# Routed groups of a mixture-of-experts layer taken two at a time on TensorE, with gathers ahead of scatters

## Chip, cores and metric

The kernel runs on one core of a Trainium2 chip. The metric is device time in microseconds (us) of one execution; lower is better. TensorE's granted clock in the profiled execution is 0.993 of 2.4 GHz on average, and 1.00 in the stage that the change touches.

## The reference

A small vision tower with one layer: 16 images of 96x96, 37 tokens each (T = 592 tokens, width 256), float32. Patch embedding, a transformer block (16 heads, low-rank projections), a layer norm, and then the feed-forward part that matters here, a mixture of experts:

```
logits = xt @ gate_w.T                      # 15 experts
scores = softmax(logits);  topk_w, topk_idx = top_k(scores, 3);  topk_w /= sum(topk_w)
h = xt @ fc1_w[e].T + fc1_b[e]              # 256 -> 512, halves xh and g
a = gelu(g) * xh * geglu_mult[e]            # 256
yexp = a @ fc2_w[e].T + fc2_b[e]            # 256 -> 256
y = sum over the token's 3 experts of topk_w * yexp
ys = a shared expert of width 512, for every token
out = layernorm(x + y + ys)
```

## The kernel before

Everything up to the shared expert runs first (about 138 us). Then come the routed experts. Their 1776 token rows are sorted by expert into 42 half groups of 64 rows; two half groups make a group of 128 rows, so there are NT = 21 groups. The upper half of group i belongs to expert i (from group 15 on, to a copied set of weights), the lower half to an expert that is read from a table at run time. Each group goes through a chain over all engines:

1. POOL, `gather(i)`, L556 to L562: an indirect DMA reads the group's 128 token rows from DRAM into one of NXG = 6 buffers `xg` (inside embed_sb). It waits until the transpose of group i-6 has read the buffer.
2. PE, `tile_transposed(i)`, L1641 to L1647: two transposes of 128x128 float32 into PSUM bank 6 + i % 2.
3. ACT, `tile_in(i)`, L742 to L747: copies them to `xT` (in cT), two buffers.
4. PE, `first(i)`, L1663 to L1681: the first products. Two bf16 matmuls add the bias (96 rows x 64 columns, 512 moving), then eight float32 matmul instructions (128x64, 512 moving; the instructions of the two halves stand in different columns of the array and run side by side) into bank 4 + i % 2.
5. ACT, `gate(i)`, L749 to L753: gelu of half of the result.
6. DVE, `gated(i)`, L1228 to L1233: the product with the other half into `a_r` (in h1), two buffers; it waits until the transpose of group i-2 has read the buffer.
7. PE, `gated_transposed(i)`, L1683 to L1691: two transposes into bank 2 + i % 2.
8. DVE, `gated_in(i)`, L1235 to L1240: copies them to `aT` (in cT), two buffers; it waits until the second products of group i-2 are done.
9. PE, `second(i)`, L1693 to L1701: the second products, eight float32 instructions (128x64, 256 moving) into bank i % 2.
10. ACT, `tile_out(i)`, L755 to L759: copies the result to one of NYS = 4 buffers `ys` (in ln_mem); it waits until the scatter of group i-4 has left the buffer.
11. POOL, `scatter(i)`, L564 to L572: an indirect DMA writes the rows to `y_dram`, sorted by token.

Each engine has its own queue, in order, written out by hand; semaphores tie them together. The queues before are: PE takes in each turn first(i), second(i-2), tile_transposed(i+1), lower_expert(i+1), gated_transposed(i-1) (L1706 to L1718). `lower_expert(i)` (L1651 to L1653) is a value load: PE's sequencer reads an expert's number from SBUF into a register that addresses the weights. ACT takes gate(i), tile_out(i-2), tile_in(i+1) and, from i = 4 on, one `diagonal` (L761 to L765, a scaled copy of the identity for the final sum; L767 to L777). DVE takes gated(i), gated_in(i-1), and in the first three turns parts of the softmax of the gate (`softmax_end`, `weigh`, `choose_weights`; L1242 to L1252). POOL takes six gathers, then scatter(i), gather(i+6) (L576 to L581).

SP copies the weights for the last six groups (L453 to L457); copy k waits for the first products of group 2k, and first(15) waits for all copies (L1673). After the last scatter, SP reads all rows back from y_dram (L459 to L461), PE adds them up over the diagonals (L1720 to L1737), and DVE and ACT do the final layer norm.

## Time and profile before

| | us |
|---|---|
| median of 3 runs | 240.78 (240.02 to 243.75) |
| the profiled execution, its own time | 240.42 |
| its span, first to last instruction | 238.6 |
| PE busy | 220.6 (92%) |
| ACT busy | 95.5 |
| DVE busy | 98.5 |
| POOL busy | 107.1 |
| bias of group 0 to bias of group 20 | 138.84 to 213.77 |

Times in the rows are counted from the first instruction of the span. PE is TensorE's matmul stream and PEld its weight loads; PEldq is the sequencer in front of them. Ends of matmuls are modelled, so a start is a firmer number than an end. A float32 transpose or matmul stands under the line of its helper: L344 is every matmul, L1646 the transposes of gathered rows, L1690 those of the gated rows. `stage`, `f1v`, `xn`, `h` and `f2u` as weights in the rows of the last groups are the copies. 1.8 us of the profiled time lie outside the span.

### The profile page before, as it was taken

What the parts mean: (1) busy time and instruction counts of PE and PEld (TensorE: products, weight loads), DVE (VectorE), ACT (ScalarE), POOL (GpSimd) and SP (SyncE); (2) the same over time, 40 slices, a digit from 0 to 9 for tenths busy, and PEclk for the clock granted to TensorE, in tenths of its full rate; (3) what the DMA queues carried; (4) which work ended last, traced back from release to release, by engine and by line L of the source; (5) the groups of instructions that cost most, each with busy time, mean ns of one, the idle gap of its engine ahead of it and who ended that gap; (6) DMA issues with size and microseconds to landing.
All of it is one profiled execution on the core that took longest, in us unless ns stands there. A gap on an engine that the chain in (4) does not pass through costs nothing.

```text
span 238.6 us, 4515 instructions
## 1 busy us (share of the span) xinstructions
PE 220.6 (92%) x1605; PEld 142.4 (60%) x1605; DVE 98.5 (41%) x261; ACT 95.5 (40%) x215; POOL 107.1 (45%) x149
## 2 busy tenths in 40 slices
PE   7999899888997899999999989999999999999991
PEld 4776577677776577777877734444444444444670
DVE  3155432679962521243678845222222212121043
ACT  2003546476782694345231523243433424333132
POOL 0130028388420699999900360644546464333100
PEclk9999999999997999999999999999999999999999
DMA  7999999000004980000110040398435222201552
GB/s 234 400 347 390 347 413 414 28 4 3 3 0 150 420 355 0 3 0 3 44 58 0 26 110 3 99 325 320 168 119 198 66 69 66 66 25 44 180 193 81
DMA packets 11648, 34.43 MB, mean 144 GB/s; under 512 B 2426, under 2 KB 4139, under 8 KB 11628
## 3 DMA queue, kind: packets, MB, share of 16 engines
q1 hardware_dynamic: 9612, 28.65, 32.0%
q0 software_dynamic: 2016, 5.51, 7.6%
q8 instruction: 13, 0.21, 0.4%
q14 instruction: 7, 0.06, 0.1%
HBM read 25.43 MB, written 4.01 MB: 123 GB/s over the span
## 4 chain that ended last, share of the span: by engine, by line
PE 84%; ACT 8%; issue 3%; DVE 2%; DMA 2%; ACTq 0%
PE ps L344 76%; ACT cT L746 3%; PE ps L1646 3%; PE ps L1445 2%; DMA embed_sb<-embed 2%; ACT pair_mem L679 1%; ACT pair_mem L673 1%; PE ps L1455 1%; DVE ln_mem L848 1%; ACT xn L605 0%; PE ps L1563 0%; PE ps L1399 0%; PE ps L1327 0%; DVE ln_mem L835 0%; ACT ln_mem L588 0%
## 5 line engine op out<-in xcount | busy, mean ns | idle before, releaser
L344 PE MATMUL ps<-wres,cT 128*64 (+1 forms) x360 | 63.8, 465 | 0.4 <-DVE cT L1239 0.4
L344 PEld LDWEIGHTS ps<-wres,cT 128*64 128x64 f32 (+1 forms) x360 | 26.2, 131 | 29.2 <-issue 24.2
L568 POOL DMA_INDIRECT y_dram<-ln_mem,dest_i x21 | 20.8, 989 | 40.0 <-ACT ln_mem L759 39.7
L559 POOL DMA_INDIRECT embed_sb<-x_dram,gather_i x21 | 20.7, 986 | 20.5 <-DVE gather_i L1164 14.4
L1232 DVE TENSOR_TENSOR h<-ps,h 128x256 f32<-128x256 f32 x21 | 8.9, 425 | 47.1 <-issue 31.0
L529 POOL TENSOR_SCALAR wres<-wres,mult 128x256 f32<-128x256 f32 x30 | 27.1, 915 | 0.0
L753 ACT ACTIVATE h<-ps 128x256 f32<-128x256 f32 x21 | 8.1, 385 | 42.4 <-PE ps L344 38.3
L357 POOL TENSOR_TENSOR wres<-wres,cst_sb 128x148 f32<-128x148 f32 x24 | 10.9, 481 | 23.2 <-DVE wres L868 20.8
L344 PE MATMUL ps<-h,stage 128*128 128x296 f32 x64 | 17.7, 417 | 0.0
L344 PE MATMUL ps<-bias_t,fac_mem 96*64 96x512 bf16 x42 | 8.5, 403 | 5.8 <-ACT cT L746 5.3
L490 POOL TENSOR_TENSOR wres<-wres,cst_sb 128x111 f32<-128x111 f32 x32 | 11.1, 378 | 6.1 <-PE ps L1455 6.1
L344 PE MATMUL ps<-embed_sb 128*128 128x288 f32 (+1 forms) x63 | 13.5, 375 | 0.2 <-DMA embed_sb<-embed 0.2
L344 PEld LDWEIGHTS ps<-h,stage 128*128 128x128 f32 x64 | 11.7, 190 | 3.2
L1239 DVE COPY cT<-ps 128x256 f32<-128x256 f32 x21 | 8.8, 425 | 11.1 <-PE ps L1690 11.1
L344 PE MATMUL ps<-xn,wres 128*128 128x296 f32 x48 | 13.1, 419 | 0.0
L759 ACT ACTIVATE ln_mem<-ps 128x256 f32<-128x256 f32 x21 | 8.1, 385 | 11.2 <-PE ps L344 10.7
L344 PEld LDWEIGHTS ps<-embed_sb 128*128 128x128 f32 (+1 forms) x63 | 10.3, 179 | 3.7 <-DMA embed_sb<-embed 0.8
L598 ACT ACT_TABLE_LOAD x9 | 11.5, 1283 | 1.3 <-DVE eps_t L800 1.1
L699 ACT ACTIVATE embed_sb<-ps,vec_sb 128x296 f32<-128x296 f32 x16 | 7.9, 504 | 9.0 <-PE ps L344 9.0
L344 PE MATMUL ps<-embed_sb,f1v 128*128 128x296 f32 x32 | 10.8, 424 | 0.2 <-ACT embed_sb L699 0.2
L344 PEld LDWEIGHTS ps<-xn,wres 128*128 128x128 f32 x48 | 8.8, 190 | 3.2 <-issue 0.9
L344 PE MATMUL ps<-embed_sb,f2u 128*128 128x296 f32 x32 | 10.3, 412 | 0.0
(194 smaller groups left out, 393.0 us busy)
## 6 DMA issues: line engine op xcount, KB each, us to landing
wres<-experts SPq DMA_DIRECT2D x15, 768.0 KB, 13.6
embed_sb<-embed SPq DMA_DIRECT2D x6, 416.0 KB, 5.4
wres<-ut SPq DMA_DIRECT2D x3, 768.0 KB, 9.2
stage<-shared SPq DMA_DIRECT2D x2, 771.0 KB, 13.6
wres<-y_dram SPq DMA_DIRECT2D x4, 384.0 KB, 4.5
stage<-wres SPq DMA_DIRECT2D x2, 512.0 KB
f1v<-fc_v SPq DMA_DIRECT2D x1, 512.0 KB
f2u<-fc_u SPq DMA_DIRECT2D x1, 512.0 KB
```

The costliest lines, as they stand in the source:

```text
L344: return nc.tensor.matmul(o, w, x, start=start, stop=stop)
L357: return eng.tensor_tensor(kblk[:, par, u, c], kT[:, c, bass.ds(p * (2 * S) + u * S, S)].unsqueeze(1).to_broadcast([P, HR, S]), cst[:, C_B ...
L490: pool.tensor_tensor(vst[:, par, c, u].rearrange("p (r s) -> p r s", r=G3), vT[:, c, bass.ds(p * (2 * S) + u * S, S)].unsqueeze(1).to_broa ...
L529: pool.tensor_scalar(w[:, f * D:(f + 1) * D], w[:, f * D:(f + 1) * D], factors[:, f:f + 1], None, ALU.mult).then_inc(scaled, 1)
L559: pool.indirect_dma_start(out=xg[:, i % NXG], out_offset=None, in_=x_dram[:, :], in_offset=bass.IndirectOffsetOnAxis(ap=gather_i[:, column ...
L568: pool.indirect_dma_start(out=y_dram[:, :], out_offset=bass.IndirectOffsetOnAxis(ap=dest_i[:, column(i):column(i) + 1], axis=0), in_=ys[:, ...
L598: nc.scalar.activation(warm_t[:, i:i + 1], eps_t[:, 0:1], function)
L699: nc.scalar.activation(hm[:, f], ps[:, HM_BANK + g % 2, 0:HT], ACT.Gelu_apprx_tanh, bias=vec[:, C_FC1B + f:C_FC1B + f + 1]).then_inc(hm_do ...
L753: nc.scalar.activation(gel_r[:, i % 2], ps[:, 4 + i % 2, F:2 * F], ACT.Gelu).then_inc(ge_done, 1)
L759: nc.scalar.activation(ys[:, i % NYS], ps[:, i % 2, 0:D], ACT.Copy).then_inc(ys_done, 1)
L1232: nc.vector.tensor_tensor(a_r[:, i % 2], ps[:, 4 + i % 2, 0:F], gel_r[:, i % 2], ALU.mult).then_inc(a_done, 1)
L1239: nc.vector.tensor_copy(aT[:, i % 2].rearrange("p f s -> p (f s)"), ps[:, 2 + i % 2, 0:F]).then_inc(at_done, 1)
```

## The change

The four queues are rewritten to take two groups in a turn. PE takes first(j), first(j+1), then tile_transposed of j+2 and j+3 (each followed by its lower_expert), gated_transposed of j-2 and j-1, and second of j-4 and j-3, for j = 0, 2, ..., 20. The second products thus come two pairs behind the first ones, where they were two groups behind. After the loop come second(18), gated_transposed(20) after second(19), and second(20). ACT, DVE and POOL follow in the same order. On POOL gather(i+6) now stands ahead of scatter(i-4), where scatter(i) stood ahead of gather(i+6). No operation is added or taken away.

```diff
--- before.py
+++ after.py
@@ -576,9 +576,12 @@
             for i in range(NXG):
                 gather(i)
             for i in range(NT):
-                scatter(i)
                 if i + NXG < NT:
                     gather(i + NXG)
+                if i >= 4:
+                    scatter(i - 4)
+            for i in range(NT - 4, NT):
+                scatter(i)
@@ -765,16 +768,18 @@
             tile_in(0)
-            for i in range(NT):
-                gate(i)
-                if i >= 2:
-                    tile_out(i - 2)
-                if i + 1 < NT:
-                    tile_in(i + 1)
-                if 4 <= i < 4 + TOPK * TT:
-                    diagonal(i - 4)
-            tile_out(NT - 2)
-            tile_out(NT - 1)
+            tile_in(1)
+            for j in range(0, NT, 2):
+                for i in range(j, min(j + 2, NT)):
+                    gate(i)
+                for i in range(j + 2, min(j + 4, NT)):
+                    tile_in(i)
+                for i in range(max(j - 4, 0), max(j - 2, 0)):
+                    tile_out(i)
+                for q in range(max(j - 4, 0), min(max(j - 2, 0), TOPK * TT)):
+                    diagonal(q)
+            for i in range(NT - 3, NT):
+                tile_out(i)
             warm(ACT.Sqrt)
@@ -1239,15 +1244,15 @@
-            for i in range(NT):
-                gated(i)
-                if i >= 1:
-                    gated_in(i - 1)
-                if i == 0:
+            for j in range(0, NT, 2):
+                for i in range(j, min(j + 2, NT)):
+                    gated(i)
+                for i in range(max(j - 2, 0), j):
+                    gated_in(i)
+                if j == 0:
                     softmax_end()
-                if i == 1:
                     weigh()
-                if i == 2:
+                if j == 2:
                     choose_weights()
             gated_in(NT - 1)
@@ -1701,20 +1706,23 @@
             pe.wait_ge(own_done, 2)
-            lower_expert(0)
-            tile_transposed(0)
-            for i in range(NT):
-
-                first(i)
-                if i >= 2:
-                    second(i - 2)
-                if i + 1 < NT:
-                    tile_transposed(i + 1)
-                    lower_expert(i + 1)
-                if i >= 1:
-                    gated_transposed(i - 1)
+            for i in range(2):
+                lower_expert(i)
+                tile_transposed(i)
+            for j in range(0, NT, 2):
+
+                for i in range(j, min(j + 2, NT)):
+                    first(i)
+                for i in range(j + 2, min(j + 4, NT)):
+                    tile_transposed(i)
+                    lower_expert(i)
+                for i in range(max(j - 2, 0), j):
+                    gated_transposed(i)
+                for i in range(max(j - 4, 0), max(j - 2, 0)):
+                    second(i)
+            second(NT - 3)
+            second(NT - 2)
             gated_transposed(NT - 1)
-            second(NT - 2)
             second(NT - 1)
```

## Rows read from the trace of the kernel before

**Rows 1.** The page, busy time (share of the span) and instructions of each engine.
```profile
PE 220.6 (92%) x1605; PEld 142.4 (60%) x1605; DVE 98.5 (41%) x261; ACT 95.5 (40%) x215; POOL 107.1 (45%) x149
```

**Rows 2.** Chain that ended last, routed stage: start us, us, what.
```profile
148.61 2.99 PE ps L344 x18
...
213.33 0.39 ACT cT L746
213.77 2.99 PE ps L344 x18
```

**Rows 3.** Timeline of group 19: start us, us, engine line op, [idle before <- releaser].
```profile
209.94 0.41 PE L344 MATMUL ps<-bias_t,fac_mem 96*64 96x512 bf16 x2 [0.26 <-ACT cT L746]
210.18 0.59 PE L344 MATMUL ps<-wres,cT 128*64 x1
...
211.89 0.38 PE L344 MATMUL ps<-wres,cT 128*64 x1
...
212.54 0.38 PE L344 MATMUL ps<-wres,cT 128*64 x1
...
212.86 0.44 PE L1646 MATMUL ps<-cst_sb,embed_sb 128*128 128x128 f32 x2
...
213.13 0.38 PE L1690 MATMUL ps<-cst_sb,h 128*128 128x128 f32 x2
213.33 0.38 ACT L746 ACTIVATE cT<-ps 128x256 f32<-128x256 f32 x1
```

**Rows 4.** One line's instructions, the gated transposes: duration ns min/median/max.
```profile
L1690 PE MATMUL ps<-cst_sb,h x42: 272/273/328, 144.1 to 217.1; 128*128 128x128 f32 x42
```

**Rows 5.** Timeline of the end of the stage, columns as in rows 3.
```profile
216.69 0.66 PE L1690 MATMUL ps<-cst_sb,h 128*128 128x128 f32 x4
...
217.16 0.76 DVE L1239 COPY cT<-ps 128x256 f32<-128x256 f32 x2 [0.38 <-PE ps L1690]
...
217.73 0.42 PE L344 MATMUL ps<-wres,cT 128*64 x1 [0.39 <-DVE cT L1239]
...
218.64 0.38 PE L344 MATMUL ps<-wres,cT 128*64 x1
...
219.72 0.38 ACT L759 ACTIVATE ln_mem<-ps 128x256 f32<-128x256 f32 x1 [0.48 <-PE ps L344]
...
220.23 0.71 PE L344 MATMUL ps<-cst_sb,hs 128*128 128x128 f32 x4
220.79 0.97 POOL L568 DMA_INDIRECT y_dram<-ln_mem,dest_i  x1 [0.30 <-issue]
...
220.87 0.69 PE L344 MATMUL ps<-b_sb,comb 17*128 17x256 f32 x2
```

**Rows 6.** Timeline of the first groups, columns as in rows 3.
```profile
137.99 0.38 PE L1646 MATMUL ps<-cst_sb,embed_sb 128*128 128x128 f32 x2
...
138.84 0.41 PE L344 MATMUL ps<-bias_t,fac_mem 96*64 96x512 bf16 x2 [0.47 <-issue]
...
140.90 0.44 PE L1646 MATMUL ps<-cst_sb,embed_sb 128*128 128x128 f32 x2
141.02 0.38 ACT L753 ACTIVATE h<-ps 128x256 f32<-128x256 f32 x1 [2.23 <-issue]
```

**Rows 7.** PE's sequencer, the value load L1653: all, group 0, group 20 (last row).
```profile
L1653 PEldq TENSOR_LOAD <-owner_i x21: 297/309/942, 136.9 to 210.7; - x21
...
L1653 PEldq SEQ_ASSERT  x1: 32/32/32, 137.7 to 137.7; - x1
...
L1653 PEldq SEQ_ASSERT  x1: 18/18/18, 211.4 to 211.4; - x1
```

**Rows 8.** One line's instructions, POOL's gathers: duration ns min/median/max.
```profile
L559 POOL DMA_INDIRECT embed_sb<-x_dram,gather_i x21: 945/973/1169, 134.2 to 203.4; - x21
```

**Rows 9.** SP's last issue of a weight copy, columns as in rows 3.
```profile
178.34 0.51 SPq L457 DMA_DIRECT2D h<-wres  x1
```

**Rows 10.** DMA of 138 to 238.6 us in 40 equal slices.
```profile
GB/s 101 111 7 1 12 108 197 345 293 380 348 131 64 325 143 52 333 136 52 52 104 57 54 104 52 52 103 54 0 59 52 0 52 104 232 314 184 55 101 88
```

## Prediction

> **What bounds the kernel now.** I read the page first: PE is busy for 92% of the span, every other engine for less than half [rows 1]. So only time in which PE stands or changes over can be gained, unless another queue starts to hold PE back. Next, the chain of work that ended last. In the routed stage it repeats one pattern, 18 matmul instructions on PE (2.99 us), two transposes, then the copy L746 on ACT (0.39 us), then PE again. From group 3 (148.61) to group 20 (213.77) there are 17 periods, 65.16 / 17 = 3.83 us each [rows 2]. ACT is thus on the path once per group, though it is 40% busy.
>
> The timeline of one group shows where the 3.83 us go [rows 3]. From the bias at 209.94 to the first product 0.24 us; four pairs of first products to 211.89, 1.71 us; four pairs of second products, whose last starts at 212.54, so 0.65 / 3 = 0.215 us each and 0.86 for all. That is 2.81 us of products. The transposes start at 212.86, 0.10 us later than the next product would have (212.54 + 0.215 = 212.76). The copy L746 starts at 213.33, ends at 213.71, and the next bias starts at 213.77. PE had idled 0.26 us by then. Sum: 2.81 + 0.10 + 0.44 (two transposes) + 0.03 + 0.38 + 0.06 = 3.82.
>
> **The change part by part.** I count in the time t of a turn of two groups, 0 at bias(j).
>
> *Products.* The same instructions: 2 x (0.24 + 1.71) = 3.90 us for first(j) and first(j+1), 2 x 0.86 = 1.72 us for two seconds [rows 3]. No gain, no loss.
>
> *Change-over to the transposes.* One per pair instead of one per group, 0.10 us each [rows 3].
>
> *Transposes.* Four in a row take 0.66 us from the first start to the last end [rows 5], one of them 0.27 [rows 4], so the fourth starts 0.39 after the first. The first is followed after 0.17, later ones after 0.11 (in rows 3 the third starts 0.27 after the first and the two after it span 0.38 - 0.27 = 0.11). Eight in a row: 0.17 + 6 x 0.11 = 0.83 from first to last start. What was 2 x 0.66 becomes 1.10 to the last end.
>
> *Change-over from the transposes to second().* Rows 3 show none of these without a wait. It lies between 0.11 us after the last transpose's start (no cost at all) and 0.27 + 0.15 = 0.42 (all run out, and a first weight load that nothing hides, as the wait of 0.14 from DVE's end, 217.59, to PE's start, 217.73, in rows 5). A near row is the end of the kernel: from float32 matmuls of 128 moving columns on 128 rows, started at 220.23 and spanning 0.71, the last starts at about 220.67 and the 17-row matmul at 220.87 [rows 5], 0.20 us. I take 0.21, 0.10 above no cost, like the other direction. From second() to a bias, and from first() to a bias, no tile width changes; I take 0 and at most 0.10 for each.
>
> The Trainium skill (TensorEngine Tiling, Key Properties) says that a change of tiling mode, not just of the tile, drains TensorE. Rows 3 nearly agree, since the transpose starts 0.06 before the modelled end of the product ahead of it (212.54 + 0.38). By that rule the way back would cost 0.27 instead of 0.21, and the forecast would be some 0.5 us later; the rule also speaks for the change, which halves the number of drains.
>
> *Sum.* 3.90 + 0.10 + 0.83 + 0.21 + 1.72 = 6.76 us for two groups, against 7.66. I use 6.77. With both ends of the unknowns it is 6.66 to 7.18.
>
> *What hides the ACT copies.* gate(j+1) follows its bias by 2.18 us [rows 6], t = 1.95 + 2.18 = 4.13 to 4.52. tile_in(j+2) then runs to 4.93, tile_in(j+3) to 5.32. bias(j+2) comes at 6.77, so 1.8 us of cover: the wait of 0.26 per group is gone. Four gated transposes and two seconds are that cover. Where it is missing, at j = 0 and j = 2, the wait stays (below).
>
> *DVE.* gated(j) needs `a_r` free, that is gated_transposed(j-2), which now stands behind first(j+1): its end is t = 4.00 + 0.61 + 0.27 = 4.88, so gated(j) runs to 5.34 (0.43 each, rows 5) and gated(j+1) to 5.80. First(j+2) at 6.77 needs the former. gated_in(j-2) waits for second(j-4), t = 5.04 + 1.08 = 6.12, and ends at 6.55; gated_in(j-1) ends 0.6 us into the next turn. Their readers come at 5.04 of the turn after. What is late next is gated(j) with 1.4 us of slack.
>
> *POOL.* A DMA costs 0.97 us plus 0.30 between two [rows 5]; two gathers and two scatters per pair are 4 x 1.28 = 5.1 us of 6.77; with the longest gather in all four places, 1.17 + 0.30 [rows 8], 5.9. gather(j+9) waits behind scatter(j-2), which waits for tile_out(j-2) in the next turn, at t = 6.77 + 6.5 = 13.3; its transposes run in turn j+8, four turns on, at t = 4 x 6.77 + 4 = 31. tile_out(i) needs a buffer scattered two turns earlier. Cost 0.
>
> *Value loads.* From 136.9 to 137.7 one takes PE's sequencer 0.8 us [rows 7]. Now two stand close together, 1.6 us in the sequencer with 0.22 us of transposes between. Before, the load for group 20 was over at 211.4 [rows 7] while its transposes started at 212.86 [rows 3]: the sequencer was 1.4 us ahead of the array with one load done. In the new order it is let go at t = 5.32 of the turn before, when xT is filled, and needs its next transposes out 5.4 us later. I take 0.
>
> *Weight copies.* The last is issued at 178.34 [rows 9], and the DMA falls back from 333 GB/s within the slices to 183.3 [rows 10], 5 us later. In the new order first(10) is done near 172, and first(15), which waits for the copies, comes near 185.4 (turn times as below: bias(10) at 149.6 + 3 x 6.77, bias(15) at 149.6 + 5 x 6.77 + 1.95). Cost 0.
>
> *Start.* The order is now load(0), transposes(0), load(1), transposes(1), first(0). transposes(0) start at 137.99 and bias(0) at 138.84 [rows 6]; the load for group 0 ends at 137.7 [rows 7], so load(1) ends near 138.5, transposes(1) run from about 138.8, and bias(0) comes at 139.15. That costs 0.3 us (0 to 0.6, the gather of group 1 being about as late). First(0), first(1): to 143.05. Four transposes from 143.15; tile_in(2) waits for gate(1) and ends at 144.08; bias(2) at 144.13, 0.4 us of wait. First(2), first(3), eight transposes from 148.14; gated_transposed(0) ends at 149.02, gated(2) on DVE at 149.48, and first(4) waits for it: bias(4) at 149.6. From there every turn is full: bias(20) at 149.6 + 8 x 6.77 = 203.8, against 213.77 [rows 2].
>
> *End.* In exchange more is left: before, two seconds and a pair of transposes, now second(16) to second(20). After bias(20): first 1.95, change-over 0.10, four transposes to the last start 0.39, 0.21 back: second(16) starts at 206.42. Four seconds, 3.44; change-over 0.10; gated_transposed(20), 0.44; gated_in(20), 0.03 + 0.43 + 0.14 [rows 5], which nothing covers now, where second(19) covered it before. second(20) starts at 211.0, against 218.64 [rows 5]: 7.6 us earlier. POOL's last five scatters come 0.86 us apart but take 1.28: the first can start at 206.42 + 1.08 + 0.38 + 0.03 = 207.9, the last at 213.0, against 220.79 [rows 5]: 7.8 us earlier. The reading back and the final sum start from these two, so all moves by 7.7. Profiled execution: 240.42 - 7.7 = 232.7. The median of the runs lies 0.36 above that execution, so 233.1.
>
> **The rivals.**
>
> 1. *The change-overs cost more.* Transposes to second at 0.42 and 0.10 at each of two other edges: up to 0.4 us per pair, 9 pairs, 3.7 us more, 236.8. For it: the 17-row matmuls near the end, which start 0.20 apart from their neighbours. Against it: bias to first products, another change of rows, costs 0.24 - 0.21 = 0.03 [rows 3].
>
> 2. *The wait only changes its name.* The 0.26 us return elsewhere, as PE's wait for gated(j), which now hangs on a transpose late in the turn, or on second() for gated_in. If both savings are lost, 9 turns x 0.9 = 8 us come back: 240.8. For it: exactly this happens at j = 2. Against it: 1.4 us of slack in full turns.
>
> 3. *Slower: the value loads.* They stand in PE's own queue. If the sequencer can't run further ahead than the array's last few instructions, both are exposed, 1.6 us per pair over 8 full turns, 12.8 us: 245.9. It decides once the sequencer's lead at tile_transposed(j+2) is under 1.6 us. Against it: a lead of 1.4 us left after a load, that is over 2 us before it [rows 3, 7].
>
> The Trainium skill (TensorE: Matmul & The Clock Gate, the table of the engine) gives the engine's queue a depth of 64. The products of one group are fewer instructions than that, and by this rule rival 3 would not come up at all.
>
> **How the numbers follow.** The forecast has 0.80 (its own range 231.9 to 234.6), rival 1 0.12, rival 2 0.05, rival 3 0.03. A measurement of this kernel can tell about 2% from no change, 4.8 us, so faster means under 236.0. The forecast and a third of rival 1 lie there: 0.84. Within 2%: most of rival 1 and rival 2, 0.13. Slower: 0.03. The range for 8 in 10 goes from 231.0 (no change-over cost at all, 9 x 0.11 = 1.0 us, a free start, and the spread of the runs) to 236.4 (most of rival 1).
>
> **What would show it right or wrong.** Right: bias starts of even groups 6.7 to 6.9 us apart from group 4 on, no idle time of PE put down to L746 but at groups 2 and 4; transposes in runs of eight, 1.1 us; second() 0.2 us after the last transpose starts; last scatter near 213. Rival 1 shows as turns of 7.0 us or more with no wait behind them, rival 2 as PE idle behind DVE's L1232 or L1239, rival 3 as gaps after the transposes put down to issue, next to a TENSOR_LOAD. The forecast is wrong if turns are longer than 7.1 us or if the last scatter is later than 217.

## The result, and the profile after

| | before | after |
|---|---|---|
| runs beside each other, median (lowest to highest) | 242.26 us (240.02 to 243.9) | 232.69 us (232.08 to 233.6) |
| profiled execution | 240.42 us | 232.10 us |
| its span | 238.6 us | 230.3 us |
| mean granted TensorE clock in it | 0.993 | 0.993 |
| first transposes of the routed stage (us in the span) | 137.99 | 136.13 |
| last scatter starts | 220.79 | 212.53 |
| from there to the end of the span | 17.81 | 17.77 |

Ratio 0.9676, 95% interval 0.9621 to 0.9731: faster. (The ratio leaves out two runs of before, 243.75 and 243.9 us, that count as slow beside its fastest, so it is not the quotient of the two medians.) The forecast was 233.1 us, the median 0.4 below it. But the sum behind it is not that good, and the table shows where. The stage that the change rewrites, from the first transposes to the last scatter, went from 82.80 to 76.40 us, 6.40 less, where the forecast's terms, unrounded, give 7.75 (its text has 7.8, and 7.7 for the whole time). The other 1.86 us lie ahead of it, in code that the change doesn't touch, and they made up for the difference.

The windows view, here the stretch from 65 to 120 us of both kernels (us, busy time and instructions of PE, PEld, DVE, ACT, POOL, granted clock, DMA share, GB/s), first before, then after:

```profile
65.00:120.00 55.00, 52.93 (x358) 39.93 (x358) 22.06 (x59) 28.33 (x54) 41.16 (x44) 0.97 0.27 106
```

```profile
65.00:120.00 55.00, 52.59 (x364) 39.53 (x362) 22.54 (x65) 28.81 (x55) 41.07 (x44) 1.00 0.28 111
```

In the execution of before the granted clock was at its lower level (1.2 GHz) from 74.7 to 78.1 us, in that of after it was not. At half speed for 3.4 us PE does some 1.7 us less, about the 1.86 that are to be explained. The other kernels' profiles agree: of all 12 profiled executions, the five with such a stretch near 74 to 78 us reach the first transposes at 137.99 to 138.38, the seven without it at 135.70 to 136.99. (After has its lower stretch near the end of the span, at no cost: last scatter to end 17.77 against 17.81, so the equal mean clocks of the table mean little.) Such stretches come and go between executions of one kernel, so I compare the kernels below by the stage alone, and give the times beside it.

The stage itself as the chain of work that ended last shows it (start us, us, what):

```profile
141.85 0.95 issue
142.81 4.09 PE ps L344 x20
...
147.35 0.68 ACT cT L749 x2
...
160.34 1.53 another core or an unknown queue
...
162.12 0.39 ACT cT L749
...
173.41 0.59 PE ps L1651 x4
173.99 0.44 PE ps L1695 x4
174.43 5.75 PE ps L344 x36
180.18 0.59 PE ps L1651 x4
```

Where before had a copy on ACT in every period [rows 2], the chain of a full turn is now PE alone: eight transposes, 36 matmul instructions, 180.18 - 173.41 = 6.77 us. PE waits at three places, ahead of bias(2) at 142.81, bias(4) at 148.35 and bias(8) at 162.57, and these views name ACT or `issue` for it. PE's waits in the stage (what waited <- for what: us in all, times, longest), before:

```profile
PE ps L344 <- ACT cT L746: 5.3, 20, 0.5
```

and after:

```profile
PE ps L344 <- issue: 1.0, 1, 1.0
PE ps L344 <- ACT cT L749: 0.9, 2, 0.5
PE ps L344 <- DVE cT L1244: 0.6, 1, 0.6
```

Which of them ACT really ended is told by the starts. first(j+2) waits for two things, the copy tile_in(j+2) on ACT and gated(j) on DVE. Where the copy is the last, as at all the waits of before, the bias follows its end by 0.05 us; so it does at bias(2) (142.75 to 142.81). At bias(4) and bias(8) the copies had ended 0.61 and 0.34 us earlier, and what ended 0.15 us before the bias was gated(2) and gated(6):

```profile
147.78 0.76 DVE L1237 TENSOR_TENSOR h<-ps,h 128x256 f32<-128x256 f32 x2 [3.04 <-PE ps L1695]
...
148.35 0.41 PE L344 MATMUL ps<-bias_t,fac_mem 96*64 96x512 bf16 x2 [0.46 <-ACT cT L749]
```

(Two groups' instructions are merged in the first line; each takes about 0.4 us, and gated(2) ends at 148.21.) So these two waits are DVE's, and the copy on ACT bounds only the first.

The change-over, in the timeline of a full turn of after:

```profile
173.34 0.66 PE L1651 MATMUL ps<-cst_sb,embed_sb 128*128 128x128 f32 x4
...
173.81 0.66 ACT L749 ACTIVATE cT<-ps 128x256 f32<-128x256 f32 x2
173.83 0.60 PE L1695 MATMUL ps<-cst_sb,h 128*128 128x128 f32 x4
174.32 0.42 DVE L1237 TENSOR_TENSOR h<-ps,h 128x256 f32<-128x256 f32 x1 [4.25 <-PE ps L1695]
...
174.36 1.95 PE L344 MATMUL ps<-wres,cT 128*64 x16
...
176.14 0.39 PE L344 MATMUL ps<-bias_t,fac_mem 96*64 96x512 bf16 x2
```

The last transpose starts at 173.83 + 0.60 - 0.27 = 174.16, second(j-4) at 174.36: 0.20 us, where 0.21 was taken. The eight transposes run from 173.34 to 174.43, 1.09 us (1.10 taken). The copy that the bias at 176.14 needs is the first of the two; it ends at 174.20, 1.94 us ahead. gated(10) on DVE starts at 174.32, 0.11 after the modelled end of the transposes that it waits for, and ends 1.39 us ahead of the bias; as the bias follows it by 0.15 where it has to wait, that is a slack of 1.24 us, the smaller of the two.

The end of the stage, and the turn of group 6 in which bias(8) came late, in the same timeline:

```profile
159.13 0.66 PE L1651 MATMUL ps<-cst_sb,embed_sb 128*128 128x128 f32 x4
...
159.62 0.60 PE L1695 MATMUL ps<-cst_sb,h 128*128 128x128 f32 x4
...
161.84 0.66 ACT L749 ACTIVATE cT<-ps 128x256 f32<-128x256 f32 x2 [1.15 <-remote]
162.00 0.76 DVE L1237 TENSOR_TENSOR h<-ps,h 128x256 f32<-128x256 f32 x2 [6.14 <-remote]
...
162.57 0.41 PE L344 MATMUL ps<-bias_t,fac_mem 96*64 96x512 bf16 x2 [0.47 <-ACT cT L749]
...
207.44 0.97 POOL L568 DMA_INDIRECT y_dram<-ln_mem,dest_i  x1 [2.16 <-ACT ln_mem L762]
...
212.53 0.97 POOL L568 DMA_INDIRECT y_dram<-ln_mem,dest_i  x1 [0.30 <-issue]
```

The first of the transposes at 159.13 end, by the model, at 159.5, and PE goes on in order to the gated ones and to second(). Yet ACT gets to copy them only at 161.84, and DVE gets to gated(6), which waits for the gated transposes of group 4 (modelled end 160.00), only at 162.00: both start within 0.2 us of each other, 2.3 and 2.0 us behind their transposes, as if PE's signals for them had been held back. I call this a late signal below, and count it by tile_in unless DVE is named. Over the whole stage tile_in starts 0.04 to 0.16 us after the modelled end of its transposes, except for groups 2 and 3 (0.74 and 1.94) and groups 8 and 9 (2.28 and 2.34). In before it is 0.04 at all 21 groups.

### The profile page after: what moved, and what is told of

Read it like the earlier page. It is cut to its first block, busy times and chain, and to the rows that moved or that the text cites. A ratio compares the mean times of both kernels' runs of the same rounds, so it can differ in the third digit from the quotient of the medians.

```text
span 230.3 us, 4515 instructions
## 1 busy us (share of the span) xinstructions
PE 215.0 (93%) x1605; PEld 140.8 (61%) x1605; DVE 97.1 (42%) x261; ACT 94.5 (41%) x215; POOL 106.7 (46%) x149
## 4 chain that ended last, share of the span: by engine, by line
PE 83%; ACT 5%; DVE 3%; DMA 3%; issue 3%; another core or an unknown queue 1%; POOL 1%; ACTq 0%
PE ps L344 75%; PE ps L1450 3%; PE ps L1651 2%; DMA embed_sb<-embed 2%; PE ps L1695 2%; ACT pair_mem L682 2%; ACT pair_mem L676 1%; DMA embed_sb<-x_dram,gather_i 1%; PE ps L1460 1%; DVE ln_mem L853 1%; ACT xn L608 1%; POOL embed_sb L559 1%; PE ps L1568 0%; ACT cT L749 0%
## 5 line engine op out<-in xcount | busy, mean ns | idle before, releaser
L344 PE MATMUL ps<-wres,cT 128*64 (+1 forms) x360 | 65.9, 468 | 0.6 <-DVE cT L1244 0.6
L1237 DVE TENSOR_TENSOR h<-ps,h 128x256 f32<-128x256 f32 x21 | 8.3, 422 | 45.5 <-PE ps L1695 24.5
L344 PE MATMUL ps<-embed_sb 128*128 128x288 f32 (+1 forms) x63 | 12.8, 362 | 0.3 <-DMA embed_sb<-embed 0.3
L344 PEld LDWEIGHTS ps<-embed_sb 128*128 128x128 f32 (+1 forms) x63 | 9.8, 172 | 3.5 <-DMA embed_sb<-embed 0.8
L1244 DVE COPY cT<-ps 128x256 f32<-128x256 f32 x21 | 8.7, 422 | 7.8 <-PE ps L344 7.8
```

The source lines that it names most:

```text
L344: return nc.tensor.matmul(o, w, x, start=start, stop=stop)
L1237: nc.vector.tensor_tensor(a_r[:, i % 2], ps[:, 4 + i % 2, 0:F], gel_r[:, i % 2], ALU.mult).then_inc(a_done, 1)
L1244: nc.vector.tensor_copy(aT[:, i % 2].rearrange("p f s -> p (f s)"), ps[:, 2 + i % 2, 0:F]).then_inc(at_done, 1)
```

## The experiments

The late signals were the one thing that the forecast had no room for, and there were five questions: do they come back, and at the same groups (a0_again); how much of the gain is the cover of the wait and how much the pairing (e1, e3); does PE's sequencer bound anything (e4); what calls the late signals up (e5, e6, e7, e8); and what the depth of two pairs and the new order on POOL are for (e2, e9). A, B and C in the expectations are the readings that the run was to tell apart. "The stage" is the time from the first transposes of the stage to the last scatter, in the profiled execution.

### a0_again: the changed kernel once more, unaltered

> The changed kernel once more, unaltered, for a second profile. In its first profile two pieces were longer than predicted: bias(0) to bias(2) took 5.61 us (4.98 predicted) and bias(6) to bias(8) 7.42 (6.77), both with ACT starting a copy 1 us or more after its inputs were there. Theory A (a stall tied to the order of the instructions): both come back at the same groups, and the stage from the first transpose (L1651) to the last scatter (L568) is again 76.4 us. Theory B (an accident of one execution): at least one of them is gone or sits at another group, and the stage is 75.2 to 76.0 us.

Stage 76.33 us (76.40 the first time). The turns, from bias(0) on: 5.89, 5.54, 6.79, 7.11, 6.79, 6.77, 6.78, 6.78, 6.77, 6.56. Both long turns come back at the same places, the first and the fourth, as A has it, though not to the same size (5.61 and 7.42 at first), and groups 12 and 13 get a late signal (1.55 and 1.61 us) that costs nothing. The fourth turn also shows that the copy on ACT is not its cause: tile_in(8) starts 0.04 us after its transposes here, while gated(6) starts 1.69 us after its own, and the bias waits for it, this time by the profile's own word:

```profile
163.96 0.75 DVE L1237 TENSOR_TENSOR h<-ps,h 128x256 f32<-128x256 f32 x2 [5.82 <-PE ps L1695]
...
164.53 0.41 PE L344 MATMUL ps<-bias_t,fac_mem 96*64 96x512 bf16 x2 [0.15 <-DVE h L1237]
```

Median of 5 runs 234.48 us against 240.39 before, ratio 0.9812, interval 0.9723 to 0.9901. With an equal stage the time is still 1.8 us above that of the first series. The windows view of the last part of the program says why for the profiled execution (span 235.2), in a0_again and then in after:

```profile
215.00:235.00 20.00, 15.36 (x62) 10.89 (x60) 4.80 (x20) 4.02 (x11) 0.47 (x1) 0.83 0.38 131
```

```profile
213.00:230.00 17.00, 12.27 (x62) 8.78 (x60) 4.81 (x20) 4.08 (x11) 0.50 (x1) 0.91 0.44 154
```

Its clock was lower (0.83) behind the stage, where the last scatter to the end took 20.71 instead of 17.77 us, and lower between 65 and 120 us as in before (0.97). So whole times tell kernels of this family apart by 2 us at best. The stage repeats to 0.1 us here, though partly because its two stalls moved in opposite directions (the first turn 0.28 longer, the fourth 0.31 shorter).

### e1_seconds_last: before, with second() moved behind the transposes

On ACT, tile_in(i + 1) changes places with tile_out(i - 2); on PE:

```diff
                 first(i)
-                if i >= 2:
-                    second(i - 2)
                 if i + 1 < NT:
                     tile_transposed(i + 1)
                     lower_expert(i + 1)
                 if i >= 1:
                     gated_transposed(i - 1)
+                if i >= 2:
+                    second(i - 2)
```

> The kernel before, one group at a time, with second(i-2) moved behind the two pairs of transposes. It covers the wait for ACT's copy L746 and leaves one change-over each way per group. Theory A (the gain has two parts, the wait and the halved change-overs): a group costs 2.81 + 0.10 + 0.39 + 0.21 = 3.51 us instead of 3.83; 18 x 0.32 = 5.8 us less than before, about 0.976 of it, and 1 to 2 us slower than the changed kernel per its full turns. Theory B (pairing is worth nothing beyond the wait): 3.39 us per group, as in the changed kernel. Theory C (the wait comes back elsewhere when one group covers it): 3.7 us or more.

Stage 77.37 us; median 234.26 us, ratio 0.9819, interval 0.9713 to 0.9924. One period of the timeline:

```profile
177.91 0.39 PE L344 MATMUL ps<-bias_t,fac_mem 96*64 96x512 bf16 x2
178.13 1.89 PE L344 MATMUL ps<-wres,cT 128*64 x8
179.94 0.44 PE L1646 MATMUL ps<-cst_sb,embed_sb 128*128 128x128 f32 x2
180.22 0.38 PE L1690 MATMUL ps<-cst_sb,h 128*128 128x128 f32 x2
180.53 1.08 PE L344 MATMUL ps<-wres,cT 128*64 x8
181.45 0.39 PE L344 MATMUL ps<-bias_t,fac_mem 96*64 96x512 bf16 x2
```

3.54 us a group, and no wait at the bias: second() is cover enough for ACT's copy. Nothing else of the change is in this kernel, neither the pairs nor POOL's order, and it already has 82.80 - 77.37 = 5.43 of the 6.40 us. Taking two groups at a time adds the last 1.0. In whole time even that can't be seen: in the same series the changed kernel took 234.48 us (a0_again), this one 234.26. The period is near that of theory A (3.51). It shows no late signal: tile_in starts 0.04 us after its transposes throughout.

### e3_changeover_back: the changed kernel, with two more changes of width per turn

```diff
                 for i in range(j + 2, min(j + 4, NT)):
                     tile_transposed(i)
                     lower_expert(i)
+                if j >= 4:
+                    second(j - 4)
                 for i in range(max(j - 2, 0), j):
                     gated_transposed(i)
-                for i in range(max(j - 4, 0), max(j - 2, 0)):
-                    second(i)
+                if j >= 4:
+                    second(j - 3)
```

> The changed kernel with second(j-4) moved between the gathered rows' transposes and the gated ones: one more change-over each way per turn, all else equal. Theory A (change-overs cost what the rows say: 0.10 into transposes, 0.10 out of them, 0.06 more for the first transpose): turns of 6.78 + 0.26 = 7.04 us, 9 x 0.26 = 2.3 us slower than the changed kernel. Theory B (change-overs cost nothing, only covered waits matter): 6.78 us and the same time. Theory C (TensorE runs empty at each): 7.2 us or more.

Stage 77.77 us, full turns 7.08 us; median 234.79 us, ratio 0.9811, interval 0.9659 to 0.9964.

```profile
180.35 0.66 PE L1651 MATMUL ps<-cst_sb,embed_sb 128*128 128x128 f32 x4
180.93 1.08 PE L344 MATMUL ps<-wres,cT 128*64 x8
181.95 0.66 PE L1695 MATMUL ps<-cst_sb,h 128*128 128x128 f32 x4
182.53 1.08 PE L344 MATMUL ps<-wres,cT 128*64 x8
...
187.43 0.66 PE L1651 MATMUL ps<-cst_sb,embed_sb 128*128 128x128 f32 x4
```

Nothing waits here; a turn is longer by 7.08 - 6.78 = 0.30 us, for one more way into the transposes and one more way out of them. So 0.30 us a turn is what the pairing by itself saves: e1, with 2 x 3.54 = 7.08 us for two groups, pays the same. The stage is only 1.4 us longer than the changed kernel's, not the 2.3 of theory A: eight turns of 0.30 are 2.4, but the fourth has no stall here, which gives back 0.65 (the signals of groups 8 and 9 are 1.62 and 1.66 late and cost nothing), and the rest is at the two ends. The Trainium skill (TensorEngine Tiling, Key Properties) says that a change of tiling mode drains TensorE. The runs agree as far as such a change costs time, 0.30 us for both ways together beyond what the instructions would take in a row; that this time is a drain is not shown.

### e4_loads_doubled: a second value load in front of each

In lower_expert() on PE:

```diff
+                pe.value_load(owner_i[0:1, at:at + 1], min_val=0, max_val=E - 1)
```

> The changed kernel with every value load of PE's sequencer done twice, four per turn (3.2 us of the sequencer, more while the weight copies run, when one load was seen to take up to 1.24 us). Theory A (the sequencer is far enough ahead of the array): turns stay at 6.78 us from group 8 on and the stage from first transpose to last scatter at 76.4 us, but for the first two loads, which stand ahead of the first transposes and cost 0.8 us or so before them. Rival 3 of the prediction (the loads are exposed): turns of 8 us and more, 10 us over the stage.

The turns: 6.26, 5.55, 6.80, 7.24, 7.37, 6.77, 6.78, then 6.78 but for the last, 6.55. Stage 78.13 us; median 235.68 us, ratio 0.9776, interval 0.9690 to 0.9863. In all full turns but one four loads, 4 x 0.8 = 3.2 us in the sequencer, cost nothing (the 7.24 us of the fourth are a late signal's, see below). They cost at the start, 1.73 us from the first transposes to bias(0) instead of 1.05, where the array has no work ahead to hide them, and once more in the fifth turn, 7.37 us, whose copies on ACT start on time. There the weight copies run, one of its four loads takes 1.12 us instead of the median 0.30, and PE stands between the two rows of transposes:

```profile
167.96 0.66 PE L1651 MATMUL ps<-cst_sb,embed_sb 128*128 128x128 f32 x4
...
169.00 0.63 PE L1696 MATMUL ps<-cst_sb,h 128*128 128x128 f32 x4 [0.39 <-issue]
169.56 0.65 PE L344 MATMUL ps<-wres,cT 128*64 x4
```

From the first transpose to second() it is 1.60 us instead of 1.02 (173.34 to 174.36 above), and 0.58 of the turn's extra 0.59 us are that. It is the sign that rival 3 named, a gap put down to `issue` next to a TENSOR_LOAD, in one turn and at twice the loads. With the loads of the changed kernel no turn shows it, though single loads take up to 0.82 us there and 1.24 in a0_again. So rival 3 has fallen for this kernel, but the lead of the sequencer is not without end.

### e5_no_copies: the changed kernel without the weight copies

```diff
-                sp.dma_start(copy_w1[k], wres[:, bass.ds(e * WC, W1C)]).then_inc(ld_copy, 16)
-                sp.dma_start(copy_w2[k], wres[:, bass.ds(e * WC + W1C, W2C)]).then_inc(ld_copy, 16)
...
-                yield slice(TM, P), w1(i, c) if i < E else copy_w1[i - E][:, c * 2 * F:(c + 1) * 2 * F]
+                yield slice(TM, P), w1(i % E, c)
...
-                if i == E:
-                    pe.wait_ge(ld_copy, 32 * NCOPY)
```

SP's copies go, and first() and second() read wres itself. The upper halves of groups 15 to 20 take the weights of experts 0 to 5 in place of the chosen ones; the instructions on PE are as many as before.

> The changed kernel with the twelve weight copies left out; the upper halves of groups 15 to 20 take the weights of experts 0 to 5 instead, so this part of the result is another one. In all profiles so far PE's signals (xT, gated, first products done) came to ACT and DVE up to 2 us behind the modelled ends near 142 to 147 us and near 158 to 162 us. Theory A (the copies' DMA traffic or their semaphore updates hold up the second stall): the turn from bias(6) to bias(8) falls from 7.1 to 7.4 us to 6.78, the first stall stays; stage 0.5 us shorter. Theory B (it has nothing to do with the copies): 7.1 us or more there again.

Stage 75.98 us, turns 5.92, 5.55, 6.79, 6.78, 6.77, 6.78 and so on: the fourth turn, 7.42 and 7.11 in the changed kernel, is a full turn like the others. The first still has its 5.9, and the signals of groups 2 and 3 are late (1.06 and 1.99 us), no others. The timeline at the place of the second stall:

```profile
161.43 0.66 PE L1649 MATMUL ps<-cst_sb,embed_sb 128*128 128x128 f32 x4
161.90 0.66 ACT L747 ACTIVATE cT<-ps 128x256 f32<-128x256 f32 x2
...
164.23 0.39 PE L344 MATMUL ps<-bias_t,fac_mem 96*64 96x512 bf16 x2
```

This is one profile, with whole times of two runs only (232.79 and 236.87 us). But all five other profiles with second() two pairs behind and with the copies (after, a0_again, e3, e4, e6) have late signals behind group 4, and this one has none. So the second stall hangs on the copies, the first on something else.

### e6_late_gathers: the gathers behind the first six held back at the start

In gather(i) on POOL:

```diff
+                if i == NXG:
+                    pool.wait_ge(f1_mm, 4)
```

> The changed kernel with gathers 6 to 9 held back on POOL until first(3) is done (before the change they stood behind the first scatters). Theory A (these four gathers, which the new order lets run at 141 to 145 us, hold up PE's signals at groups 2 and 3): bias(0) to bias(2) falls from 5.6 to 5.9 us to 5.0 to 5.1, stage 0.6 us shorter than 76.4. Theory B (no connection): 5.6 us or more there, and 76.4.

The first turn falls to 4.91 us (forecast 4.98), and no signal of groups 2 and 3 is late. In the other runs of this order the first turn is 4.91 us plus the delay of tile_in(2) beyond its usual 0.04: with 0.70 us of it 5.61 (after), with 0.98 5.89 (a0_again), with 1.36 6.26 (e4). So the first stall has to do with POOL's row of gathers, which in the changed kernel runs on past the first six at one every 1.25 us. But the late signals move rather than go: 2.34 and 2.40 us at groups 6 and 7, 1.30 at group 11, with turns of 7.49 and 7.31. As in a0_again, DVE is the one that PE waits for: bias(6) and bias(10) follow gated(4) and gated(8) by 0.15 us. Theory A is right about the first turn and wrong about the stage: 76.25 us, as good as unchanged; median 235.64 us, ratio 0.9707, interval 0.9610 to 0.9804.

### e2_one_pair_back and e7_one_pair_back_no_copies: second() one pair behind

PE as in the diff, ACT and DVE in the same order, and on POOL gather(i + 6), then scatter(i - 2). e7 is e2 with the weight copies left out as in e5, groups 15 to 20 computed as there.

```diff
                 for i in range(j, min(j + 2, NT)):
                     first(i)
+                for i in range(max(j - 2, 0), j if j < NT - 1 else j - 1):
+                    second(i)
                 for i in range(j + 2, min(j + 4, NT)):
                     tile_transposed(i)
                     lower_expert(i)
-                for i in range(max(j - 2, 0), j):
+                for i in range(j, min(j + 2, NT)):
                     gated_transposed(i)
-                for i in range(max(j - 4, 0), max(j - 2, 0)):
-                    second(i)
...
```

> Pairs, but with the second products one pair back: first(j), first(j+1), second(j-2), second(j-1), transposes of j+2, j+3, then of j, j+1. The eight transposes themselves must cover ACT's copy. Theory A (a turn costs its PE work as long as every copy is covered, and depth only adds filling and emptying): turns of 6.78 us as in the changed kernel, and 1 to 2 us less at the two ends, so 0.992 to 0.996 of the changed kernel. Theory B (the second products are needed as cover): PE waits for L746 or its counterpart in each turn, 7.0 us or more, slower than the changed kernel by 1 to 3 us.

> The kernel with the second products one pair back (turns of 6.63 to 7.56 us, the long ones while the copies run), with the copies left out and the weights of experts 0 to 5 in groups 15 to 20, so that part of the result is another one. Theory A (its eight transposes leave ACT's copy 0.1 us of cover, and the copies' traffic makes signals later than that): without copies all full turns are 6.6 to 6.8 us and the stage is 75.0 us or less, shorter than the changed kernel's 76.4. Theory B (the order itself is too shallow): turns stay above 6.9.

e2: stage 77.15 us, turns of 6.42 to 7.56; median 236.59 us. e7: stage 76.81, turns mostly 6.91 to 6.95; median of two runs 235.87 us, ratio 0.9810, interval 0.9701 to 0.9920. Both come out nearer to B, the order is too shallow (e2's shortest turns, 6.42 to 6.97 us, are not the 7.0 or more that B had). In e2's timeline:

```profile
156.20 0.66 PE L1650 MATMUL ps<-cst_sb,embed_sb 128*128 128x128 f32 x4
...
157.61 0.66 ACT L749 ACTIVATE cT<-ps 128x256 f32<-128x256 f32 x2 [2.63 <-PE ps L1650]
158.04 0.41 PE L344 MATMUL ps<-bias_t,fac_mem 96*64 96x512 bf16 x2 [0.75 <-ACT cT L749]
```

The signal is late by some 1 us and PE stands at the bias for 0.75. With second() ahead of the transposes only the four gated ones cover the copies, and that is 0.11 us: a turn without a late signal takes 6.74 us and its copy ends 0.16 ahead of the bias. All lateness beyond that is paid; in e7 a signal that comes 0.3 us late makes a turn 0.18 longer. In the changed kernel the second products of two groups lie there, 1.7 us. Without the copies (e7) the signals of groups 2 and 3 are still 2.3 us late, those of groups 6 and 7 0.8, and from there to group 17, as long as gathers run, 0.31 to 0.42; from group 18 on it is 0.04 to 0.10. The change's second pair of depth is thus worth 0.8 us of the stage (77.15 - 76.40, and without the copies 76.81 - 75.98), and what it buys is cover against late signals.

### e8_seconds_last_new_pool: e1 with POOL's new order

On top of e1's edits:

```diff
             for i in range(NT):
-                scatter(i)
                 if i + NXG < NT:
                     gather(i + NXG)
+                if i >= 4:
+                    scatter(i - 4)
+            for i in range(NT - 4, NT):
+                scatter(i)
```

> One group at a time with second(i-2) behind the transposes (e1, where ACT's tile_in always started 0.04 us after its transposes and the stage took 77.4 us), and with POOL's queue of the changed kernel: gather(i+6) ahead of scatter(i-4), so that gathers 6 to 9 run early. Theory A (POOL's queue, its run of ten gathers above all, is what makes PE's signals late): tile_in starts 0.5 us or more late at some of groups 2 to 13, as in the changed kernel. Theory B (the pairs on PE are what it takes): 0.04 us at every group, 3.54 us per group, 77.4 us.

Stage 77.38 us, 3.54 a group, tile_in 0.04 us after its transposes at every group: the same as e1. Median 234.53 us, ratio 0.9721, interval 0.9637 to 0.9804. POOL's order alone neither helps nor harms, and it doesn't call up late signals. In the profiles at hand they come only with pairs on PE.

### e9_one_pair_back_old_pool: pairs, with POOL's old order

On top of e2's edits:

```diff
             for i in range(NT):
+                scatter(i)
                 if i + NXG < NT:
                     gather(i + NXG)
-                if i >= 2:
-                    scatter(i - 2)
-            for i in range(NT - 2, NT):
-                scatter(i)
```

> Pairs with the second products one pair back (e2: turns of 6.63 to 7.56 us, 77.15 us), with POOL's queue of the kernel before: scatter(i), then gather(i+6). Theory A (POOL's queue makes the signals late): tile_in starts within 0.1 us of its transposes at groups 2 and 3, bias(0) to bias(2) falls from 6.42 to 5.1 us, the stage to 75 or 76 us. Theory B: late signals at the same places, 77 us.

Median 249.08 us (246.21 to 251.71), against 240.00 (238.04 to 243.57) before: 9 us slower than the kernel before the change, and 12.5 more than e2 took in its series. Both theories missed that: the signals are on time and bias(0) to bias(2) takes 5.38 us (A had 5.1), but the stage takes 91.13 us, with turns of up to 11.62. PE's waits and, below them, the timeline of one:

```profile
PE ps L1647 <- DMA embed_sb<-x_dram,gather_i: 7.8, 6, 2.2
```

```profile
175.10 0.45 PE L1647 MATMUL ps<-cst_sb,embed_sb 128*128 128x128 f32 x2
...
177.78 0.44 PE L1647 MATMUL ps<-cst_sb,embed_sb 128*128 128x128 f32 x2 [2.24 <-DMA embed_sb<-x_dram,gather_i]
```

The transposes wait for their gathers. But standing explains less than half of the 14 us over e2's stage. The rest goes with the clock: in this kernel's stage alone, of all twelve profiled ones, the granted clock falls to its lower level, from 157.92 to 164.75, 178.40 to 181.81 and 205.71 to 209.12 us. The windows view of the first of these stretches, columns as above:

```profile
157.92:164.75 6.83, 5.86 (x18) 2.35 (x20) 0.85 (x2) 1.56 (x6) 3.66 (x4) 0.50 0.52 190
```

Each begins during or up to 1.7 us after a wait of PE for a gather (2.18, 2.24 and 1.44 us long). Over the stage PE is idle for 9.98 us, against 3.78 in e2, and busy for 81.15 against 73.37 with the same 469 instructions: 6.2 us more of standing and 7.8 of slower work.

That a gather comes late follows from the queues. In the old order gather(i+6) stands behind scatter(i), which waits for the end of second(i); with the pairs that comes too late for transposes taken two groups at once. So the edit on POOL, which costs and gives nothing in e8, is what the pairs stand on. (As PE stands so much in e9, its signals being on time doesn't show that POOL's order as such makes them late elsewhere.) With second() two pairs behind it is more than that: tile_transposed(j+6), in the turn of first(j+4), stands ahead of second(j) on PE, while its gather would stand behind scatter(j) on POOL, a circle. For that reason e9 is built on e2 and not on the changed kernel; the circle itself is read from the queues and no run shows it.

## Why the prediction was right, step by step

**A full turn: right.** Forecast 6.77 us; measured 6.77 to 6.80 in six of the seven turns from bias(4) to bias(18). Each term stands: 0.20 us from the last transpose to second() (0.21), 1.09 for eight transposes (1.10), no cost at the edges from second() to a bias. Rival 1, dearer change-overs, has fallen: it needed up to 0.4 us a pair on top of the forecast's terms, and e3 prices both ways together at 0.30, where these terms gave 0.26 to 0.27. The seventh turn, 7.42 us, is beyond the 7.1 that the forecast had named as a sign of being wrong, and the last scatter, counted from the first transposes, comes 1.4 us later than forecast.

**The step "What hides the ACT copies": right but for the first turn.** 1.8 us of cover were forecast and 1.9 are there in every full turn without a late signal, so the wait for the copy is gone from them. In the first turn, where nothing covers it, the forecast had 0.4 us of wait and took the copy to start as soon as its transposes and gate(1) were done; in all 21 groups of before it started 0.04 us behind the transposes. It started 0.74 us behind them, and bias(0) to bias(2) took 5.61 instead of 4.98 us.

**The step "DVE ... gated(j) with 1.4 us of slack": the size was right, and it wasn't enough.** 1.24 us are there. In the fourth turn gated(6) started 2.00 us behind its transposes, 1.89 later than in a full turn, and 1.89 - 1.24 = 0.65 is what the turn is too long (7.42 against 6.77). The same sum gives the other long turns: 1.58 us of delay in a0_again, 0.34 over (7.11); 1.72 in e4, 0.48 over (7.24); 1.95 and 1.78 in e6, 0.71 and 0.54 over (7.49 and 7.31). This is rival 2 in small and in its own terms, PE waiting for gated(j), "which now hangs on a transpose late in the turn". What neither it nor the forecast had is the reason, a signal that comes late, and 0.65 + 0.63 = 1.3 us in all are the failed term of the sum.

**The start: right but for the late signal.** From the first transposes to bias(0) 1.07 us, 1.15 forecast; bias(2) to bias(4) 5.54 (5.47).

**The last turn: 0.22 too long.** It takes the transposes of one group only, group 20, where I counted eight full turns: 6.55.

**The end: right.** bias(20) to second(20) 7.32 us (7.24 forecast), with the wait for gated_in(20) that is named there (0.60, put down to DVE's L1244). The last five scatters start at 207.44 and every 1.27 us after, bound by POOL as forecast; the last one comes 9.51 us after bias(20) (9.28).

**Together.** The forecast had the stage at 82.80 - 7.75 = 75.05 us. Add 1.28 for the two late signals, 0.23 for the end, 0.15 for the other turns, take off 0.22 for the last turn and 0.08 for the start, and it is 76.41; 76.40 was measured. That the time came out at 232.69 all the same is due to the 1.86 us ahead of the stage, and is luck. Between executions of about equal mean clock, though of different series, the difference is the stage's: spans of 236.4 before at 1.000 and 230.2 after at 0.998, 6.2 us, and 239.4 before and 232.6 and 233.4 after at 0.985, 6.8 and 6.0 us.

**The step "POOL ... Cost 0": right as a number, incomplete as an account.** It takes only the slack of the new order and doesn't ask what the old one would have done beside pairs. e9 gives the answer for second() one pair back, 14 us of the stage, of which 6.2 are standing and 7.8 the lower clock: the reordering is no companion of the change but its condition.

**"Value loads ... I take 0": right.** No turn of the changed kernel shows a gap behind them. Twice the loads (e4) are hidden too, except at the start and in one turn beside the weight copies, 0.58 us.

**What the gain consists of.** 5.43 of the 6.40 us come from second() standing behind the transposes (e1), which covers the copy that was on the path. The pairing's fewer changes of width would give 0.30 x 9 = 2.7 us, but late signals, which only the pairs bring, take 1.3 of it, and the longer end, less what the start gains, some 0.4 (the rest of the difference), so that 1.0 is left.

## What to carry to other kernels

When one engine is at 92% and hands over to another for a short copy in each period, put independent work of that engine between the handover and its return before thinking of larger batches: here one call moved on PE and one on ACT gave 5.4 of 6.4 us of the stage, and in whole time as much as the full change. Grouping operations of one width is worth 0.3 us per avoided round trip of TensorE, but it makes a burst of demand for what feeds it: look at every queue that loads ahead, and put the loads in front of stores that wait on the consumer, or the batch costs more than it saves. And leave more cover than the trace of before asks for, since a signal that always came after 0.04 us may come after 2. Count it for every queue that a step waits for: here the copy on ACT, which the change was made for, had 1.9 us, and DVE's product with 1.24 was the one that ran out. When the profile names the engine that ended a wait for two, compare the starts: PE follows what it really waited for by 0.05 us (ACT) or 0.15 us (DVE).

## What the runs showed that was not expected

- **Late signals of PE.** With pairs on PE, and POOL issuing gathers ahead of scatters, the copies on ACT and the products on DVE started up to 2.3 us (2.66 in a0_again) after the transposes that they wait for, while PE went on with the next products. They cluster where gathers come in a row (e6 moves the first away) and where SBUF-to-SBUF weight copies run (e5 removes the second); with PE's order of single groups (e1, e8) and in e9, where POOL has its old order and PE stands for gathers, there are none. What holds them back is left open: the trace shows no wait on PE's side, and it can't be excluded that the transposes themselves ran later than the modelled ends say. It may not be PE's signals alone: within the second stall the issue of a weight copy in SyncE's queue is recorded at 0.01 us (160.26 in after) and 0.06 (e3, e4), where such issues take 0.49 us and more outside it.
- **Value loads beside copies.** A value load on PE takes 0.30 us in the median, but up to 1.24 us (a0_again; 0.94 before, 1.27 in e8) while the weight copies run. Hidden in every full turn of the changed kernel, and in all but one with the loads doubled (e4).
- **Whole times differ more than stages.** With the stage equal to 0.1 us, the changed kernel took 232.1 and 237.1 us in its two profiled executions, by stretches of lower clock ahead of and behind the stage. So the time of one execution can't order these kernels.
